# Probabilities times values: from halved fp32r products to plain fp32 by sequence

## The reference, cut to what matters

```python
q = rope(layernorm(x) @ wq); k = rope(ctx @ wk); v = ctx @ wv      # 4 query heads per kv head
attn = softmax(q @ k.T / sqrt(128) + mask)                          # per sequence, 64 x 64
out  = (attn @ v).reshape(...) @ wo
x    = x + tanh(g_xattn) * out
x    = x + tanh(g_ffn) * lora_experts(layernorm(x))                 # one of 8 experts, rank 16
```

## Time and profile before

| | before |
|---|---|
| median of 3 runs | 1066.98 us (1064.69 to 1067.41) |
| profiled execution, its own time | 1064.13 us |
| its span | 1062.3 us |
| PE busy | 1053.4 us, 99% |
| DVE busy | 873.9 us, 82% |
| ACT busy | 637.9 us, 60% |
| POOL busy | 591.7 us, 56% |
| DMA | 206.40 MB, mean 194 GB/s |

### The profile page before, as it was taken

How to read it: one execution, slowest core, us unless ns; L and a number is a source line. 1 busy time by engine, 2 the same in 40 slices (tenths; PEclk the granted TensorE clock), 3 DMA queues, 4 the chain that set the end, 5 groups by cost and what they waited for, 6 DMA issues and landing times.

```text
span 1062.3 us, 19155 instructions
## 1 busy us (share of the span) xinstructions
PE 1053.4 (99%) x6664; PEld 865.0 (81%) x6664; DVE 873.9 (82%) x1423; ACT 637.9 (60%) x1112; POOL 591.7 (56%) x518
## 2 busy tenths in 40 slices
PE   9999999999999999999999999999999999999998
PEld 7888888877788888888888888888888888888786
DVE  7876757888888888888887899888778888888897
ACT  7564466676767676767666545555555555555653
POOL 4552379897877787878764433334333443443423
PEclk9999999999999999999999999999999999999999
DMA  7868965485765656656479745563535464643102
GB/s 264 264 230 305 398 224 232 149 321 204 241 212 185 198 194 184 211 166 217 142 255 391 236 149 170 170 199 122 197 122 197 120 193 118 190 121 122 48 34 80
DMA packets 106094, 206.40 MB, mean 194 GB/s; under 512 B 8848, under 2 KB 58640, under 8 KB 100112
## 3 DMA queue, kind: packets, MB, share of 16 engines
q1 hardware_dynamic: 105424, 204.40, 57.1%
q10 hardware_dynamic: 576, 0.79, 0.2%
HBM read 122.31 MB, written 82.84 MB: 193 GB/s over the span
## 4 chain that ended last, share of the span: by engine, by line
PE 89%; DVE 6%; POOL 2%; issue 2%; ACT 1%; DMA 0%; DVEq 0%; SPq 0%; ACTq 0%
PE attn L945 30%; PE proj L877 26%; PE attn L839 8%; PE score L894 6%; PE score L839 4%; PE turned L839 4%; PE attn L930 4%; PE turned L905 2%; PE attn L932 2%; PE proj L811 1%; POOL wq_s L1838 1%; DVE o_s L1270 1%; DVE acc L1282 1%; DVE p_low L1262 1%; DVE q_r L1175 1%
## 5 line engine op out<-in xcount | busy, mean ns | idle before, releaser
L945 PE MATMUL attn<-wo_s,o_s 128*128 128x512 f32 x1524 | 375.7, 395 | 0.1
L877 PE MATMUL proj<-xB,wq_s 128*128 128x512 f32 x1344 | 332.7, 391 | 0.3 <-issue 0.3
L945 PEld LDWEIGHTS attn<-wo_s,o_s 128*128 128x128 f32 x1524 | 280.6, 188 | 58.8 <-DVE o_s L1270 1.6
L877 PEld LDWEIGHTS proj<-xB,wq_s 128*128 128x128 f32 x1344 | 251.7, 188 | 52.3 <-issue 1.0
L1863 POOL TENSOR_TENSOR rot<-rot,tab 128x512 f32<-128x512 f32 x110 | 162.2, 1475 | 146.9 <-ACT rot L1584 146.7
L1175 DVE TENSOR_TENSOR q_r<-q_r,tab 128x512 f32<-128x512 f32 x127 | 120.9, 952 | 1.6 <-ACT x_third L1584 1.4
L1633 ACT ACTIVATE o_s<-attn 128x512 fp32r<-128x512 f32 x127 | 69.5, 596 | 82.7 <-PE attn L932 81.2
L1605 ACT ACTIVATE copies<-proj 128x512 f32<-128x512 f32 x96 | 57.4, 598 | 74.1 <-PE proj L877 73.9
L1282 DVE SCALAR_TENSOR_TENSOR acc<-attn,gates_t,acc 128x512 f32<-128x512 f32 x127 | 94.9, 748 | 3.5 <-PE attn L945 0.5
L1863 POOL TENSOR_TENSOR rot_third<-rot_third,tab 128x512 f32<-128x512 f32 x40 | 61.3, 1533 | 58.6 <-ACT rot_third L1584 55.8
L1262 DVE TENSOR_TENSOR p_low<-turned,p_high 64x512 fp32r<-64x512 f32 x128 | 87.8, 686 | 5.0 <-ACT p_high L1621 2.7
(11 more groups left out here) (269 smaller groups left out, 1645.2 us busy)
## 6 DMA issues: line engine op xcount, KB each, us to landing
wq_kept<-wq_s SPq DMA_DIRECT2D x16, 1792.0 KB, 6.3
wq_s<-wq_kept SPq DMA_DIRECT2D x16, 1792.0 KB, 8.9
v_kept<-vst SPq DMA_DIRECT2D x64, 256.0 KB, 4.4
v_s<-v_kept SPq DMA_DIRECT2D x128, 128.0 KB, 5.4
wo_kept<-wo_s SPq DMA_DIRECT2D x32, 512.0 KB, 5.0
wo_s<-wo_kept SPq DMA_DIRECT2D x32, 512.0 KB, 5.4
k_kept<-kst SPq DMA_DIRECT2D x32, 256.0 KB, 2.2
wq_raw<-in_wq SPq DMA_DIRECT2D x16, 512.0 KB, 7.9
```

The costliest lines, as they stand in the source:

```text
L877: last = e.matmul(dst[:, :], wq_s[:, b % 2, A, s, kt, :], xB[:, B, mv, kt, :], start=(first and kt == 0 and m == 0), stop=(kt == 1 and m = ...
L945: last = e.matmul(out_bank(k, bp)[:, :], o_s[:, s, bp, h, :], wo_s[n % WO_SLOTS][:, m, :], start=(h == 0 and i == 0), stop=(h == GROUP - 1 ...
```

## The change

Probabilities and values stay whole. `turned` is copied once, 128 rows by 512 columns, to p_turned (ACT); prob_low, p_high, p_low, v_both, the zeros and the values' low halves go. Values are stored and fetched as they are, in one DMA each. times_values does four plain fp32 matmuls: for each pair and each twin one with the 64 rows of that sequence and 256 columns. Twin 0 writes bank attn[0] and twin 1 attn[1], so a bank now holds one sequence of both pairs, and attn_high and attn_low go by twin. project_out(k, bp) needs both, and waits for out_low of both. times_values waits for both x1 additions of the step before ahead of its first matmul. In the last steps times_values(61) stands as a whole after scores(63). Buffers are laid out anew (x_near, raw, warm share space otherwise); DVE's and ACT's lists are otherwise the same.

```diff
             def times_values(k):
                 u, s = divmod(k, SUBS)
                 tiles = [s * PAIRS + bp for bp in range(PAIRS)]
-                e.wait_ge(v_in[u % 2], 80 * (u // 2 + 1))
-                e.wait_ge(probs_low, 2 * k + 2)
-                e.wait_ge(probs_high, 3 * k + 3)
...
-                        e.wait_ge(x1_added, 2 * k - 1 + bp)
-                    b = out_bank(k, bp)
-                    for twin in range(2):
-                        e.matmul(b[:, cols[twin]], v_s[:, u % 2, twin, tiles[bp], :], p_high[:, twin, cols[bp]],
-                                 start=(twin == 0), stop=False, skip_group_check=True)
-                    e.matmul(b[:, :], v_both[:, u % 2, tiles[bp], :], p_low[:, bp].rearrange("p t n -> p (t n)"),
-                             start=False, stop=True, skip_group_check=True).then_inc(values_used, 1)
+                e.wait_ge(v_in[u % 2], 16 * (u // 2 + 1))
+                e.wait_ge(probs_copied, k + 1)
+                if k == 0:
+
+                    e.wait_ge(rope_added, ROPE_NO[JOBS[-1]] + 1)
+                elif k + 1 == STEPS:
+
+                    e.wait_ge(masked, STEPS)
+                    e.wait_ge(x1_added, 2 * k - 1)
+                else:
+                    e.wait_ge(x1_added, 2 * k)
+                for bp in range(PAIRS):
+                    cols = slice(bp * GROUP * SEQ, (bp + 1) * GROUP * SEQ)
+                    for twin, rows in enumerate(TWIN_ROWS):
+                        last = e.matmul(out_bank(k, twin)[:, cols], v_s[rows, u % 2, tiles[bp], :], p_turned[rows, cols],
+                                        start=(bp == 0), stop=(bp + 1 == PAIRS), skip_group_check=True)
+                        if bp + 1 == PAIRS:
+                            last.then_inc(values_used, 1)
 
             def project_out(k, bp):
                 G = k // (CHUNKS * SUBS)
-                e.wait_ge(out_low, 2 * k + bp + 1)
+                e.wait_ge(out_low, 2 * k + 2)
...
-            times_values(k + 1, [0])
             scores(k + 3)
-            times_values(k + 1, [1])
+            times_values(k + 1)
             turn_probs(k + 2)
...
-            def attn_low(k, bp):
-                src = out_bank(k, bp)[:, :].rearrange("p (t h q) -> p h t q", t=2, h=GROUP)
-                high, low = (o_s[:, part, bp, :, :].rearrange("p h (t q) -> p h t q", t=2) for part in (0, 1))
-                e.wait_ge(out_high, 2 * k + bp + 1)
+            def attn_low(k, twin):
+                src = out_bank(k, twin)[:, :].rearrange("p (b h q) -> p b h q", b=PAIRS, h=GROUP)
+                high, low = (o_s[:, part, :, :, TWIN_ROWS[twin]] for part in (0, 1))
+                e.wait_ge(out_high, 2 * k + twin + 1)
                 e.tensor_tensor(low, src, high.bitcast(F32), ALU.subtract).then_inc(out_low, 1)
...
-            def prob_high(k):
+            def prob_copy(k):
                 e.wait_ge(probs_turned, k + 1)
                 if k:
-                    e.wait_ge(values_used, PAIRS * k)
...
+                    e.wait_ge(values_used, 2 * k)
+                e.activation(p_turned[:, :], turned[:, :], ACT.Copy).then_inc(probs_copied, 1)
...
-                if n == ZEROS_BESIDE:
-
-                    e.wait_ge(rope_added, FOUR.stop)
-                    e.memset(p_low[:, :, :, :].bitcast(F32), 0.0).then_inc(zeros_set, 1)
...
-                for twin in range(2):
-                    for part in range(2):
-                        rows = TWIN_ROWS[twin if part == 0 else 1 - twin]
-                        e.dma_start(v_s[rows, u % 2, twin, :, :].bitcast(F32),
-                                    v_kept[index, g // 4, part, TWIN_ROWS[twin], :, cols]).then_inc(v_in[u % 2], 16)
-                e.dma_start(v_both[:, u % 2, :, :].bitcast(F32), v_kept[index, g // 4, 0, :, :, cols]).then_inc(v_in[u % 2], 16)
+                e.dma_start(v_s[:, u % 2, :, :], v_kept[index, g // 4, :, :, cols]).then_inc(v_in[u % 2], 16)
```

More of the change, by code:

```diff
@@ L643, in fetch_values @@
                     for slot in range(VST):
[L644 removed]
+                        e.wait_ge(v_stored[slot], 16 * len(range(slot, len(V_NO), VST)))
                 cols = slice(g % 4 * DH, g % 4 * DH + DH)
[L646 to L651 removed]
+                e.dma_start(v_s[:, u % 2, :, :], v_kept[index, g // 4, :, :, cols]).then_inc(v_in[u % 2], 16)
             def store_wo(n):
@@ L821, in make @@
                     else:
-                        e.wait_ge(v_low, V_NO[before] + 1)
+                        e.wait_ge(v_copied, V_NO[before] + 1)
                 here = ctxT[i % 2]
@@ L906, in turn_probs, with times_values @@
                 last.then_inc(probs_turned, 1)
[L907 to L909 removed]
+                drained[turned.name] = probs_copied, k + 1
+            def times_values(k):
                 u, s = divmod(k, SUBS)
                 tiles = [s * PAIRS + bp for bp in range(PAIRS)]
[L912 to L933 removed]
@@ L1188, in finish_job @@
                     by_cos(ROPE_NO[job], by_seq(b[:, :]), by_seq(b[:, :]))
[L1189 to L1193, removed]
             def finish_key(n):
@@ L1210, in q_sum @@
                     for slot in range(VST):
-                        e.wait_ge(v_stored[slot], 32 * len(range(slot, len(V_NO), VST)))
+                        e.wait_ge(v_stored[slot], 16 * len(range(slot, len(V_NO), VST)))
                 elif b == HEAD_PAIRS and j == 2:
@@ L1430, in _ @@
                     q_cos(*q)
-                together = k % 4 == 3 or (k, 6) in EXTRA
-                if not together:
-                    prob_low(k, 0)
                 for q in ropes[0] if k > 2 else ():
@@ L1595, in finish_job @@
                     if v >= VST:
-                        e.wait_ge(v_stored[v % VST], 32 * (v // VST))
-                    e.activation(vst[:, v % VST, 0, :], b[:, :], ACT.Copy).then_inc(v_high, 1)
+                        e.wait_ge(v_stored[v % VST], 16 * (v // VST))
+                    e.activation(vst[:, v % VST, :], b[:, :], ACT.Copy).then_inc(v_copied, 1)
             def copy_product(b, i):
@@ L1613, in exponential, with attn_high @@
                 e.activation(prob_of(k)[:, :], prob_of(k)[:, :], ACT.Exp).then_inc(exponentials, 1)
-            def prob_high(k):
+            def prob_copy(k):
                 e.wait_ge(probs_turned, k + 1)
                 if k:
-                    e.wait_ge(values_used, PAIRS * k)
-                for twin, rows in enumerate(TWIN_ROWS):
-                    e.activation(p_high[rows, twin, :], turned[rows, :], ACT.Copy).then_inc(probs_high, 1)
-                e.wait_ge(probs_high, 3 * k + 2)
-                for twin, rows in enumerate(TWIN_ROWS):
-                    last = e.activation(p_high[TWIN_ROWS[1 - twin], twin, :], p_high[rows, twin, :].bitcast(F32), ACT.Copy)
-                last.then_inc(probs_high, 1)
-            def attn_high(k, bp):
-                e.wait_ge(values_used, PAIRS * k + bp + 1)
+                    e.wait_ge(values_used, 2 * k)
+                e.activation(p_turned[:, :], turned[:, :], ACT.Copy).then_inc(probs_copied, 1)
+            def attn_high(k, twin):
+                e.wait_ge(values_used, 2 * k + twin + 1)
                 if k:
-                    e.wait_ge(out_projected, GROUP * (2 * k - 1 + bp))
-                src = out_bank(k, bp)[:, :].rearrange("p (t h q) -> p h t q", t=2, h=GROUP)
-                high = o_s[:, 0, bp, :, :].rearrange("p h (t q) -> p h t q", t=2)
-                e.activation(high, src, ACT.Copy).then_inc(out_high, 1)
+                    e.wait_ge(out_projected, GROUP * 2 * k)
+                src = out_bank(k, twin)[:, :].rearrange("p (b h q) -> p b h q", b=PAIRS, h=GROUP)
+                e.activation(o_s[:, 0, :, :, TWIN_ROWS[twin]], src, ACT.Copy).then_inc(out_high, 1)
             def expert(what, t):
```

59 lines of the change are left out of this document (20 added, 39 removed).

## The result

The changed kernel takes 1078.41 us (median of four runs, 1077.87 to 1080.11) against 1065.84 for the kernel before in the same series: ratio 1.0121, interval 1.0103 to 1.0139, or +12.6 us. The likeliest case of the prediction was no difference (1067.0); the range, 1060 to 1081, holds the time.

What follows compares the result with a forecast made beforehand. The prediction took TensorE, busy 99%, to bound the kernel through the distances between its block starts. First steps -2.0, block -4.7, looped waits 0 and tail +7.2 summed to +0.5 us, giving 1067 us; range 1060 to 1081.

Steps and rivals of the forecast that it cites:

- What bounds the kernel: Whole kernel: TensorE is busy 99%; only distances between its block starts count, other engines' work only where it waits.
- The start: First steps: the first values block 0.9 us sooner and 1.1 us of fewer late starts, together -2.0 us.
- the bounds given for the loop: Four looped steps with expert work: new waits taken as 0, between -0.5 and +1.5 us in all.
- The block: Probabilities times values: 64-row matmuls side by side in two row halves, 0.96 against 1.04 us, -4.7 us over 59 steps.
- The change into the block is there before as well: Entry to the values block after the scores: already paid in the old kernel, so nothing was added to 0.96 us.
- For the change back to the whole array 0.10: Exit from the values block: 0.10 us, read from the scores, added to 0.86 us of side-by-side matmuls.
- rival C: Values block: row halves overlap only partly, a fifth slot, 1.18 us per block, +8.3 us, total 1080; chance 8%.
- The tail: Last four steps: no products cover the projection's wait for both low halves; +7.2 us, between +4 and +9.
- rival B: Step 61: TensorE's clock falls after its stall, ten matmuls at half speed, +2.2 us, total 1069.5; chance 13%.
- the forecast: The prediction's likeliest case, whole kernel: 1064 to 1070 us; chance 42%.
- slower: Whole kernel: chance 0.34 that the change makes it slower, against 0.22 faster and 0.44 same.
- A: Values block: row halves do not overlap, 1.82 against 1.04 us, +50 us on the block, total 1122; chance 9%.

## Where the prediction held and where it failed, step by step

**What bounds the kernel**: right. TensorE's distances set the time; 210 us less on DVE and ACT gave 3.4 (2.5 and 0.9), all where TensorE had waited.

**The start**, -2.0: measured -2.5. Right, though the first block ends at 217.32 and not near 217.0, and most of the gain comes in steps 1 to 5. The 0.9 of steps 28 to 33 was inside the bounds given for the loop, with the other sign than I had feared.

**The block**, -0.08 a step: the step that failed, by 0.227 x 59 = 13.4 us, nearly the whole error. The side-by-side halves were right to the hundredth: four slots of 0.216 against 0.215. What was mis-sized is the price of the changes of mode, and it was mis-sized by where I cut. (1) "The change into the block is there before as well", I wrote, and left it out of 0.96, but it was inside the 1.04 that I compared with: the first pair is 0.320 apart and not 0.216, and before the first two matmuls took 0.33 for 0.23. That is 0.10. (2) "For the change back to the whole array 0.10" counted the way to the next block's start (0.306 for 0.216), and not that the matmul behind it then waits for its weights: 0.335 for 0.235, another 0.10. The row from which I read that change, the scores', ends at the start of the next block, and what followed was in the 1.04 that I took for the old block. 0.20 of the 0.23 are these two; where the other 0.03 goes stays open. Doubling the work, taking the split away and adding a pair of changes (0.00, -0.2 and +0.36 a step besides the columns) bear it out.

The total lies near rival C's 1080, and C's mechanism is refuted: pairs start 7 ns apart, and doubled work costs 0.21 a slot. That the range holds the time is luck as far as the block goes: its upper end had been set by C, for a reason that is not at work. A right time is no evidence for a mechanism; only the distances tell them apart.

The Trainium skill ("TensorE: Matmul & The Clock Gate", Part 3) gives 3.07 times for four row tiles. No run here has four. Two gave 2.0 times in the slots and, with the 0.34 counted in, about 1.7 times (1.73 + 0.34 against 0.86 + 0.34), so a figure for a short burst may hold the price of getting in and out.

**The tail**, +7.2: measured +8.4; right in its places and releasers. Step 60 +2.0 (forecast 1.85), step 61 +4.6 (4.5), step 62 +1.0 (0.85), step 59 -0.3 (0). The clock's fall, rival B, is real: +1.1 to +1.3 instead of its 2.2, since six matmuls and not ten were slow. The number is not fixed: in the kernel with both sequences in the same half and in the one without the split, TensorE stood for 3.8 and 4.0 us at this place, and all twelve matmuls of the projection ran at a granted clock of 0.50, in 5.49 and 5.42 us. It had 13% as an addition that excluded the forecast; it should have been a term, since the sum itself brought the stall.

**The chances**: slower had 0.34. With A and C as the only ways for the block to cost more, the chance that a fixed price was counted once where it falls twice had no place.

## What to carry to other kernels

Compare blocks with the instruction behind them included: a change between split and whole array is paid on both sides of the block, here 0.36 us for a way in and out between whole-array work and 0.2 where the work ahead was split already. Halving a block of 1 us has to gain more than that. When a result is cut another way, ask who now needs the last piece: the wait for both halves cost nothing under 2.7 us of other matmuls, and 7.0 us of waits in four steps without them, one of which was paid a second time through the clock.

## What the runs showed of the hardware

- Two 64-row matmuls in different halves start 7 ns apart, although the program issues the whole of the first one, two records, ahead of the second: the second one does not wait for the first one's second record.
- A plain fp32 matmul takes 0.216 us for each 256 columns of each of two records, with 64 rows as with 128 (0.43 for both the earlier trace rows); fp32r in row halves takes 0.117 for 256 columns.
- The granted clock was 0.50 (1.2 GHz) for the six matmuls after TensorE had stood for 4.25 us, fell likewise after 3.2 us (mean 0.69 over the 2.6 us that followed), was 0.50 for all twelve after 3.8 and 4.0 us, and stayed at 1.00 after 1.4 us. Between 1.4 and 3.2 nothing was measured in the tail.
